# A mixture-of-experts loop on one core: where the weight splits, the stores and the activation table load stand

## The chip, the cores and the metric

The kernel runs on one core of a Trainium2 chip. The metric is device time in microseconds (us) of one execution, median of three runs. The core has five engines with queues of their own: TensorE (PE), VectorE (DVE), ScalarE (ACT), GpSimd (POOL) and SyncE (SP, which here only issues DMAs).

## The reference, cut to what matters

Three stages follow each other on 8 x 64 tokens of 512 features: cross attention to 8 x 1601 context rows, linear attention with a feed-forward layer, and a mixture of experts. The change is in the third:

```python
x = hidden_states.reshape(-1, h)                       # 512 tokens, 512 features
top_w, top_i = jax.lax.top_k(x @ w_router, 2)          # two of 8 experts each
gating = zeros.at[token, top_i].add(softmax(top_w))
for ei in range(8):
    hmid = silu(x @ w0[ei]) * (x @ w1[ei])             # 512 -> 1024
    out = out + gating[:, ei:ei + 1] * (hmid @ wo[ei]) # 1024 -> 512
```

All data is float32.

## The kernel before

**Numbers.** PE multiplies a value in two parts: an upper part (`_hi`, a Copy on ACT to the float32r type) and a lower part (`_lo`, the difference, a subtraction on DVE or POOL). A full product is three matmuls: hi x hi, lo x hi, hi x lo (`product`, lines L1535, L1538, L1539). To "split" a weight unit means to make both parts from the raw tile.

**Units.** An expert has six weight units of 128 x 2048 values (1 MB): j = 0 to 3 are the halves of `w0` and `w1`, j = 4 and 5 those of `wo`. Each has a raw tile and two parts. The tiles of units 0, 1 and 2 are those that the layer before used, so the trace calls them `w_raw`, `w_hi`, `w_lo` 1, 2 and 0; those of units 3 to 5 are `e_raw`, `e_hi`, `e_lo`. `split_e` exists on ACT (L774, upper part), DVE (L1271, lower part) and POOL (L549, lower part).

**Blocks.** The 1024 pairs of token and expert are scattered by POOL (L561) to an array `slots_x` in DRAM, in slots of 32 rows by expert. Each expert ends in one long block of 128 rows; what it has beyond that is done ahead of it in short blocks of 32 rows. How many there are is data: the engines read it into registers at the head of each expert (`expert_blocks`, L328) and loop over it. In this data experts 0, 3 and 5 have one short block, expert 2 has three, the others none. A short block multiplies the raw weights in 32-row strips (L2016) and needs no parts. A long block uses the parts.

**Order on PE.** Long block (`expert_block`): units 0, 1, 2, transposes of the first hidden half (L2000), unit 3, one quarter of unit 4, transposes of the second half, transposes of the next block's rows (L1986), the rest of unit 4, unit 5. Short block: units 0, 1, 2, a transpose (L2028), unit 3, the next rows, a transpose, units 4 and 5. The first product waits for the rows' lower part, each unit for its own parts; unit 4 waits for the lower part of the first hidden half (`hmT_lo`, made by `lower_hidden`, L1445), which DVE makes after `hidden` (L1441), the product of silu and the other half.

**Order on the others.** In the long block of expert e, ACT and DVE split the units of expert e + 1 in the order 0 to 5; DVE makes the lower parts of 0 to 4, POOL that of 5. SP loads a unit of the expert after next as soon as its lower part is made (L450); unit 0 also waits until the long block has begun (`raw_free`), since short blocks read raw tiles. The first expert's units 4, 5 and 1 are split by POOL during the feed-forward layer. ACT also stores each block's result to `slots_y` in four DMAs (L884 and L853) and waits for its own copy first:

```python
                act.wait_ge(y_ready, b + 2)
                row = row_of(b) * R
                for q in range(FULL_R):
                    nc.scalar.dma_start(ys[bass.ds(row + q * R, R), :], yb[q * R:(q + 1) * R, :]).then_inc(y_stored, 16)
```

The next copy into `yb` (L840) waits for `y_stored`. The silu of a block (L826) is preceded by a load of the activation table wherever the compiler does not know which table is in place; at the head of a loop it does not.

**The end.** When all earlier blocks are stored (`prior_stored`), POOL gathers each token's two results (L571) into `yt`, whose tiles lie over `e_raw` 3 and 4, so it also waits for the lower parts 3 and 4 of the last expert. DVE adds them (`gathered_added`, L1461 and L1462), the last block's rows reach the tokens by matmuls (L2086), `last_added` (L1519) adds those, and SP stores.

## Time and profile before

| | |
|---|---|
| median of 3 runs | 681.96 us (681.34 to 682.69) |
| profiled execution | 680.1 us, its span 678.1 us |
| PE busy | 623.4 us, 92% |
| DVE, ACT, POOL busy | 61%, 57%, 36% |
| granted TensorE clock, mean | 0.974 of full |
| expert loops | from about 437 us to the end |

The span runs from the first to the last instruction. A row of the timeline gives the start in us from the span's start, the duration, the engine, the line and operation, output<-inputs, the count merged into it, and in brackets the idle time of the engine before it and who ended it. "issue" means that the engine waited for nothing that the profile shows. PE's records overlap, since matmuls are pipelined: one start to the next is what counts.

### The profile page before, as it was taken

What the parts mean: (1) busy time and instruction counts of PE and PEld (TensorE: products, weight loads), DVE (VectorE), ACT (ScalarE), POOL (GpSimd) and SP (SyncE); (2) the same over time, 40 slices, a digit from 0 to 9 for tenths busy, and PEclk for the clock granted to TensorE, in tenths of its full rate; (3) what the DMA queues carried; (4) which work ended last, traced back from release to release, by engine and by line L of the source; (5) the groups of instructions that cost most, each with busy time, mean ns of one, the idle gap of its engine ahead of it and who ended that gap; (6) DMA issues with size and microseconds to landing.
All of it is one profiled execution on the core that took longest, in us unless ns stands there. A gap on an engine that the chain in (4) does not pass through costs nothing.

```text
span 678.1 us, 12394 instructions
## 1 busy us (share of the span) xinstructions
PE 623.4 (92%) x4593; PEld 508.5 (75%) x4594; DVE 416.2 (61%) x718; ACT 386.6 (57%) x567; POOL 245.0 (36%) x170
## 2 busy tenths in 40 slices
PE   8989999999989999899999999879966979979986
PEld 7867888888868888677888888768755758757764
DVE  7775667657767456667683447817731354764796
ACT  4589989979953344420432443427843556765760
POOL 4069987878963222340000223510220020220222
PEclk9999999999999999999999999979978979979999
DMA  8515653442423332499953310239911839939944
GB/s 316 211 63 194 203 186 133 165 154 71 139 80 88 125 109 103 156 398 388 375 181 119 125 63 0 94 131 358 368 35 21 332 103 353 360 103 338 360 154 152
DMA packets 57272, 125.54 MB, mean 185 GB/s; under 512 B 5896, under 2 KB 6664, under 8 KB 54160
## 3 DMA queue, kind: packets, MB, share of 16 engines
q1 hardware_dynamic: 51584, 115.16, 47.3%
q10 hardware_dynamic: 4368, 5.64, 2.8%
q0 software_dynamic: 1280, 4.20, 1.9%
q8 instruction: 26, 0.43, 0.3%
q14 instruction: 14, 0.11, 0.0%
HBM read 102.83 MB, written 22.15 MB: 184 GB/s over the span
## 4 chain that ended last, share of the span: by engine, by line
PE 69%; issue 8%; ACT 7%; DVE 6%; ACTq 4%; POOL 3%; DMA 1%; DVEq 0%; SPq 0%; POOLq 0%
PE bank L1535 14%; PE bank L1539 14%; PE bank L1538 14%; PE bank L1551 5%; PE bank L2016 3%; PE bank L1602 3%; POOL nat_lo L501 3%; PE bank L1603 2%; PE bank L1570 2%; PE bank L1571 2%; ACT e_hi L774 2%; ACTq L884 2%; PE bank L2000 1%; ACT nat_hi L618 1%; DVE hm L1441 1%
## 5 line engine op out<-in xcount | busy, mean ns | idle before, releaser
L501 POOL TENSOR_TENSOR nat_lo<-raw,nat_hi 128x512 fp32r<-128x512 f32 x104 | 136.1, 1339 | 41.8 <-ACT nat_hi L618 41.7
L549 POOL TENSOR_TENSOR e_lo<-e_raw,e_hi 128x2048 fp32r<-128x2048 f32 x8 | 36.6, 4576 | 223.4 <-ACT e_hi L774 223.4
L925 DVE TENSOR_TENSOR ct_lo<-bank,ct_hi 128x512 fp32r<-128x512 f32 x96 | 65.9, 689 | 33.2 <-ACT ct_hi L585 32.8
L618 ACT ACTIVATE nat_hi<-raw 128x512 fp32r<-128x512 f32 x104 | 64.7, 630 | 0.0
L585 ACT ACTIVATE ct_hi<-bank 128x512 fp32r<-128x512 f32 x96 | 57.0, 596 | 9.0 <-PE bank L1551 6.8
L1441 DVE TENSOR_TENSOR hm<-bank,vectors 128x512 f32<-128x512 f32 (+1 forms) x28 | 14.5, 519 | 75.9 <-PE bank L1539 35.7
L1271 DVE TENSOR_TENSOR w_lo<-w_raw,w_hi 128x2048 fp32r<-128x2048 f32 (+1 forms) x24 | 54.6, 2298 | 9.1 <-ACT w_hi L774 9.1
L1551 PE MATMUL bank<-ident,raw 128*128 128x128 f32 x384 | 57.7, 273 | 0.3
L1551 PEld LDWEIGHTS bank<-ident,raw 128*128 128x128 f32 x384 | 46.7, 140 | 12.8 <-issue 0.9
L1535 PE MATMUL bank<-turned,w_hi 128*128 128x512 f32 (+1 forms) x144 | 53.2, 370 | 1.4 <-DVE turned L1076 1.4
L1535 PE MATMUL bank<-w_hi,turned 128*128 128x512 f32 x128 | 50.7, 396 | 2.6 <-issue 2.5
L1539 PE MATMUL bank<-turned,w_lo 128*128 128x512 f32 (+1 forms) x144 | 52.8, 367 | 0.0
L1538 PE MATMUL bank<-turned,w_hi 128*128 128x512 f32 (+1 forms) x144 | 52.7, 366 | 0.0
L1602 PE MATMUL bank<-nat_hi,pT 128*128 128x512 f32 x104 | 48.6, 467 | 1.6 <-POOL nat_lo L501 1.1
L1539 PE MATMUL bank<-w_hi,turned 128*128 128x512 f32 x128 | 49.9, 390 | 0.0
L1538 PE MATMUL bank<-w_lo,turned 128*128 128x512 f32 x128 | 49.9, 390 | 0.0
L774 ACT ACTIVATE e_hi<-e_raw 128x2048 fp32r<-128x2048 f32 x24 | 45.8, 1909 | 6.8 <-issue 6.8
L774 ACT ACTIVATE w_hi<-w_raw 128x2048 fp32r<-128x2048 f32 x24 | 46.0, 1916 | 5.2 <-issue 3.6
L523 POOL TENSOR_TENSOR w_lo<-w_raw,w_hi 128x2048 fp32r<-128x2048 f32 x6 | 27.6, 4602 | 55.8 <-ACT w_hi L672 55.8
L1535 PE MATMUL bank<-e_hi,turned 128*128 128x512 f32 x96 | 39.6, 412 | 4.1 <-DVE turned L1445 4.1
L1603 PE MATMUL bank<-nat_lo,pT 128*128 128x512 f32 x104 | 40.9, 393 | 0.0
L1570 PE MATMUL bank<-ct_hi,pw_all 128*128 128x512 f32 x96 | 39.4, 410 | 1.4 <-DVE mx L937 1.4
(292 smaller groups left out, 1484.4 us busy)
## 6 DMA issues: line engine op xcount, KB each, us to landing
raw<-in_ctx_dram SPq DMA_DIRECT2D x24, 1024.0 KB, 5.0
w_raw<-in_L_ffn_w_dram SPq DMA_DIRECT2D x24, 1024.0 KB, 7.5
e_raw<-in_L_ffn_wo_dram SPq DMA_DIRECT2D x16, 1024.0 KB, 12.7
w_raw<-in_L_attn_w_dram SPq DMA_DIRECT2D x8, 1024.0 KB, 5.8
slots_x<-zeros SPq DMA_DIRECT2D x1, 8192.0 KB, 27.7
slots_y<-zeros SPq DMA_DIRECT2D x1, 8192.0 KB, 33.1
e_raw<-in_L_ffn_w_dram SPq DMA_DIRECT2D x8, 1024.0 KB, 11.6
vectors<-slots_x ACTq DMA_DIRECT2D x13, 256.0 KB, 4.6
```

Of the source, the lines that this page charges most:

```text
L501: nc.gpsimd.tensor_tensor(nat_lo[:, j, :], raw[b % 2][:, j, :], nat_hi[:, j, :].bitcast(f32), ALU.subtract).then_inc(nat_lo_ready, 1)
L585: nc.scalar.activation(ct_hi[:, n % CR, :], src, ACT.Copy).then_inc(t_hi, 1)
L618: nc.scalar.activation(nat_hi[:, j, :], raw[b % 2][:, j, :], ACT.Copy).then_inc(nat_hi_ready, 1)
L774: nc.scalar.activation(e_hi[j][:, :, :], e_raw[j][:, :, :], ACT.Copy).then_inc(e_hi_ready[j], 1)
L925: nc.vector.tensor_tensor(ct_lo[:, n % CR, :], src, ct_hi[:, n % CR, :].bitcast(f32), ALU.subtract).then_inc(t_lo, 1)
L1271: low = nc.vector.tensor_tensor(e_lo[j][:, rows_, :], e_raw[j][:, rows_, :], e_hi[j][:, rows_, :].bitcast(f32), ALU.subtract)
L1535: mm = nc.tensor.matmul(dst, lh, rh, start=first and k == 0, stop=False)
L1538: nc.tensor.matmul(dst, lh, rl, start=False, stop=False)
L1539: mm = nc.tensor.matmul(dst, ll, rh, start=False, stop=last and k == n - 1)
L1551: mm = nc.tensor.transpose(TB[n % 3][:, i * P:(i + 1) * P], raw[b % 2][:, CH * (g // CH) + i, (g % CH) * P:(g % CH + 1) * P], ident[:, :])
L1602: nc.tensor.matmul(value_bank(b)[:, :], pT[:, j, :], nat_hi[:, j, :], start=j == 0, stop=False)
L1603: nc.tensor.matmul(value_bank(b)[:, :], pT[:, j, :], nat_lo[:, j, :], start=False, stop=j == NKT - 1).then_inc(v_step, 1)
```

## The change

- POOL splits nothing of the experts but unit 1 of the first; DVE makes all other lower parts.
- In a long block of expert e, ACT and DVE now split units 4 and 5 of expert e itself, DVE also 2 and 3 of e, and of expert e + 1 DVE makes only 0 and 1 and ACT 0 to 3. This holds for the last expert's block too.
- SP stores a long block's result, in one DMA, after it has issued the next loads; ACT stores a short block's in one DMA instead of four.
- ACT runs a silu on four columns ahead of the loops.
- Short blocks wait for the loads of raw units, not for their upper parts.
- Ahead of the loops DVE makes the four lower parts of the first rows together, and no longer splits units 2 and 3 there; the gates of the last block are made after the first `lower_hidden`.

```diff
-        POOL_FIRST = (4, 5, 1)
+        POOL_FIRST = (1,)
...
                     load_unit(e, j)
+                last_b = sp.value_load(blocks[0:1, 1, bass.ds(e - 1, 1)], min_val=0, max_val=NB - 2)
+                row = sp.value_load(place_of[0:1, bass.ds(last_b, 1)], min_val=0, max_val=ROWS - FULL_R)
+                sp.wait_ge(y_ready, last_b + 2)
+                sp.dma_start(ys[bass.ds(row * R, P), :], yb[:, :]).then_inc(y_stored, 16)
...
-            with pool.Fori(1, E - 1) as e:
-                split_e(e, POOL_UNIT)
...
-                if n in (9, 10, 11):
-                    split_e(0, (4, 5, 3)[n - 9], (xT_done, 2 * KD))
+                if n == 11:
+                    split_e(0, 3, (xT_done, 2 * KD))
...
-                act.wait_ge(y_stored, 16 * FULL_R * b + 1)
+                act.wait_ge(y_stored, 16 * b + 1)
...
-                for q in range(FULL_R):
-                    nc.scalar.dma_start(ys[bass.ds(row, R), q * P:(q + 1) * P], yb[q * R:(q + 1) * R, 0:P]).then_inc(y_stored, 16)
+                nc.scalar.dma_start(ys[bass.ds(row, R), :].rearrange("t (q c) -> q t c", q=FULL_R), yb[:, 0:P]).then_inc(y_stored, 16)
...
                 silu(b, 0)
                 if last:
-                    act.wait_ge(y_stored, 16 * FULL_R * b + 1)
+                    act.wait_ge(xg_loaded, 16 * b + 16)
+                    act.wait_ge(y_stored, 16 * b + 1)
                     nc.scalar.activation(drained[:, :], mhalf[:, :], ACT.Copy).then_inc(prior_stored, 1)
+                split_e(e, 4)
+                split_e(e, 5)
                 split(0)
                 silu(b, 1)
                 upper_hidden(b, 0)
                 split(1)
+                split(2)
                 upper_hidden(b, 1)
...
-                split(2)
                 split(3)
                 output_copied(b, D)
-                split(4)
-                act.wait_ge(y_ready, b + 2)
-                row = row_of(b) * R
-                for q in range(FULL_R):
-                    nc.scalar.dma_start(ys[bass.ds(row + q * R, R), :], yb[q * R:(q + 1) * R, :]).then_inc(y_stored, 16)
-                split(5)
...
+            nc.scalar.activation(drained[:, :], mhalf[:, 0:NT], ACT.Silu)
             act.wait_ge(slots_ready, 5)
...
-            for k in range(2, KD):
-                first_lower_rows(k)
-            split_e(0, 2)
...
+                split_e(e, 2)
+                split_e(e, 3)
                 hidden(b, 0)
...
+                split_e(e, 4)
+                split_e(e, 5)
+                lower_hidden(b, 0)
+                if last:
                     gates_made()
-                split(0)
-                lower_hidden(b, 0)
                 hidden(b, 1)
                 if last:
                     gathered_added(0)
+                split(0)
                 lower_hidden(b, 1)
                 if last:
                     return
                 lower_rows(b + 1)
                 split(1)
-                split(2)
-                split(3)
-                split(4)
-
-            split_e(0, 3)
...
-            split_e(E - 1, 5)
...
-                pe.wait_ge(e_hi_ready[j], turn_of(e, j))
+                pe.wait_ge(e_loaded[j], 16 * turn_of(e, j))
```

DVE's order in a long block, before (`hm0`, `hm1`: the two hidden halves; `turned` from banks 4 and 5: `lower_hidden`; from bank 7: `lower_rows`):

```order
L1441 TENSOR_TENSOR hm0<-bank1,vectors 128x512
L1271 TENSOR_TENSOR w_lo1<-w_raw1,w_hi1 128x2048
L1445 TENSOR_TENSOR turned<-bank4,turned 128x512
...
L1441 TENSOR_TENSOR hm1<-bank3,vectors 128x512
L1445 TENSOR_TENSOR turned<-bank5,turned 128x512
```

and with the change, from the head of the block:

```order
L1271 TENSOR_TENSOR w_lo0<-w_raw0,w_hi0 128x2048
...
L1271 TENSOR_TENSOR e_lo3<-e_raw3,e_hi3 128x2048
...
L1438 TENSOR_TENSOR hm0<-bank1,vectors 128x512
L1271 TENSOR_TENSOR e_lo4<-e_raw4,e_hi4 128x2048
L1271 TENSOR_TENSOR e_lo5<-e_raw5,e_hi5 128x2048
L1442 TENSOR_TENSOR turned<-bank4,turned 128x512
```

Two splits now stand ahead of `hm0`, two between it and the lower part that PE's unit 4 waits for, and the split of the next expert's unit 0 (`w_lo1`) has moved behind `hm1`.

ACT at the end of a short block and the head of a long one, before:

```order
L853 DMA slots_y<-yb 32x128
...
L894 UNCONDITIONAL_BRANCH
...
L826 ACT_TABLE_LOAD
L826 ACTIVATE vectors<-bank0 128x512
...
L774 ACTIVATE w_hi1<-w_raw1 128x2048
```

and with the change:

```order
L855 DMA slots_y<-yb 4x32x128
...
L894 UNCONDITIONAL_BRANCH
...
L829 ACTIVATE vectors<-bank0 128x512
...
L777 ACTIVATE e_hi4<-e_raw4 128x2048
L777 ACTIVATE e_hi5<-e_raw5 128x2048
...
L777 ACTIVATE w_hi1<-w_raw1 128x2048
```

The table load is gone from both loops (it stands once, ahead of them), four stores are one, and two splits of the block's own expert stand ahead of the next expert's first.

SP, in its loop over the experts, a piece of the difference:

```order
 L450 DMA e_raw5<-in_L0_ffn_wo_dram 128x4x512
+L466 ISA
+L466 TENSOR_LOAD blocks
+L466 ISA x2
+L467 ISA
+L467 TENSOR_LOAD place_of
+L467 ISA x2
+L468 REGISTER_ALU
+L469 ISA
+L469 DMA slots_y<-yb 128x512
```

The store of the long block stands behind the last load of an expert, and ahead of the next expert's first.

## Rows read from the trace of the kernel before

**Rows 1.** windows: us, busy us by engine (instructions), clock, DMA share, GB/s

```profile
497.00:509.00 12.00, 8.89 (x198) 7.42 (x198) 1.28 (x3) 3.51 (x9) 3.68 (x1) 0.74 0.10 27
...
520.00:529.00 9.00, 6.97 (x114) 5.48 (x115) 1.28 (x3) 2.83 (x8) 0.00 (x0) 1.00 0.15 38
```

**Rows 2.** waits of PE from 437 to 678 us: in total, times, longest

```profile
PE bank L2028 <- DVE hm L1441: 22.3, 6, 4.6
```

**Rows 3.** timeline of PE: the first instruction of seven blocks

```profile
490.71 2.83 PE L2016 MATMUL bank<-w_raw,in_last 128*32 128x128 f32 x96
...
526.21 0.50 PE L1535 MATMUL bank<-w_hi,turned 128*128 128x512 f32 x1
...
544.69 2.06 PE L2016 MATMUL bank<-w_raw,in_last 128*32 128x128 f32 x68
...
558.63 0.50 PE L1535 MATMUL bank<-w_hi,turned 128*128 128x512 f32 x1
...
577.04 0.39 PE L1535 MATMUL bank<-w_hi,turned 128*128 128x512 f32 x1
...
596.90 0.86 PE L2016 MATMUL bank<-w_raw,in_last 128*32 128x128 f32 x24
...
651.41 0.47 PE L1535 MATMUL bank<-w_hi,turned 128*128 128x512 f32 x1 [2.50 <-issue]
```

**Rows 4.** timeline of ACT (ACTq: its DMA issues): between two blocks

```profile
496.11 1.28 ACT L826 ACT_TABLE_LOAD   x1
...
505.65 1.87 ACTq L853 DMA_DIRECT2D slots_y<-yb  x4
...
507.92 1.28 ACT L826 ACT_TABLE_LOAD   x1 [3.06 <-issue]
```

**Rows 5.** timeline of PE: a transpose in the third short block of expert 2

```profile
521.54 0.33 PE L2028 MATMUL bank<-ident,hm 128*128 128x128 f32 x1 [2.90 <-DVE hm L1441]
```

**Rows 6.** one line of a tile each: ns, minimum/median/maximum

```profile
L1271 DVE TENSOR_TENSOR e_lo<-e_raw,e_hi x16: 2284/2286/2289, 439.6 to 654.3; 128x2048 fp32r<-128x2048 f32 x16
...
L774 ACT ACTIVATE e_hi<-e_raw x24: 1896/1908/1926, 383.6 to 652.3; 128x2048 fp32r<-128x2048 f32 x24
```

**Rows 7.** timeline of POOL, DVE and PE in the long block of expert 1

```profile
476.57 4.62 POOL L549 TENSOR_TENSOR e_lo<-e_raw,e_hi 128x2048 fp32r<-128x2048 f32 x1 [33.88 <-ACT e_hi L774]
...
480.22 3.11 DVE L1271 TENSOR_TENSOR w_lo<-w_raw,w_hi 128x2048 fp32r<-128x2048 f32 x1 [1.02 <-ACT w_hi L774]
...
484.08 0.47 PE L1535 MATMUL bank<-e_hi,turned 128*128 128x512 f32 x1 [1.37 <-DVE turned L1445]
```

**Rows 8.** the scatter's line of POOL, in ns

```profile
L561 POOL DMA_INDIRECT slots_x<-xn,slot_all x8: 960/1122/2382, 429.8 to 440.8; - x8
```

**Rows 9.** timeline of PE: the next rows in the first short block

```profile
447.70 1.11 PE L1986 MATMUL bank<-ident,vectors 128*128 128x128 f32 x4 [0.75 <-DMA vectors<-slots_x]
```

**Rows 10.** timeline of DVE and PE in the last block

```profile
657.17 0.69 DVE L1441 TENSOR_TENSOR hm<-bank,vectors 128x512 f32<-128x512 f32 x1 [0.56 <-PE bank L1539]
...
659.86 0.16 DVE L1451 TENSOR_SCALAR gap<-gsum 128x4 f32<-128x4 f32 x1
...
661.01 0.69 DVE L1445 TENSOR_TENSOR turned<-bank,turned 128x512 fp32r<-128x512 f32 x1
...
663.95 0.66 PE L2000 MATMUL bank<-ident,hm 128*128 128x128 f32 x4 [0.15 <-DVE hm L1441]
...
671.28 0.74 DVE L1461 SCALAR_TENSOR_TENSOR xt<-yt,gate,xt 128x512 f32<-128x512 f32 x1
```

**Rows 11.** the gathers' line of POOL, in ns, and their landing

```profile
L571 POOL DMA_INDIRECT yt<-slots_y,slot_all x8: 942/947/1453, 656.0 to 665.7; - x8
...
DMA to landing us min/median/max: 3.5/3.7/4.0
```

**Rows 12.** DMA issues, 440 to 678 us: count, KB, us to landing

```profile
e_raw<-in_L_ffn_wo_dram SPq DMA_DIRECT2D x14, 1024.0 KB, 13.7
...
slots_y<-yb ACTq DMA_DIRECT2D x24, 16.0 KB, 4.9
```

More of the change, by code:

```diff
@@ L769, in _, with split_e @@
             act.wait_ge(b1_loaded, 16)
-            def split_e(e, j, wait):
+            def split_e(e, j, wait=None):
                 act.wait_ge(e_loaded[j], 16 * turn_of(e, j))
-                act.wait_ge(*wait)
+                if wait is not None:
+                    act.wait_ge(*wait)
                 nc.scalar.activation(e_hi[j][:, :, :], e_raw[j][:, :, :], ACT.Copy).then_inc(e_hi_ready[j], 1)
@@ L1417, in _ @@
             nc.vector.tensor_copy(blocks[:, 1, :], upto_extra[:, :]).then_inc(slots_ready, 1)
-            for k in range(2):
+            for k in range(KD):
                 first_lower_rows(k)
@@ L2030, in short_down @@
             def short_down(b, e, half):
-                pe.wait_ge(e_hi_ready[4 + half], turn_of(e, 4 + half))
+                pe.wait_ge(e_loaded[4 + half], 16 * turn_of(e, 4 + half))
                 pe.wait_ge(hmT_hi_ready, 2 * b + half + 1)
```

## The prediction

> **What bounds the kernel now.** I read the page's busy shares first, then the windows of the expert loops, PE's waits there, and the timelines around each wait. PE is busy 92% of the span, so only the stretches in which it is not can give time. From 437 us on they are of four kinds.
>
> First, short blocks. PE waits 22.3 us for `hm` ahead of the first transpose of six short blocks [rows 2], 4.6 us where a long block came before. The windows show the second cost: a granted clock of 0.74 of full around the first short block of expert 2, 1.00 in the third [rows 1]. So one short block with its idle costs 558.63 - 544.69 = 13.9 us, and the three of expert 2 cost 526.21 - 490.71 = 35.5 us [rows 3]. Their work at full clock is less: the first three units take 2.83 us [rows 3], and from the first transpose to the end of the block it is 526.21 - 521.54 = 4.7 us [rows 3, 5]; together 7.5 us.
>
> Second, a long block behind a long block takes 596.90 - 577.04 = 19.9 us, one behind a short block 577.04 - 558.63 = 18.4 us [rows 3]. Row 484.08 shows most of the difference: PE waits 1.37 us for `lower_hidden`, because DVE's split ahead of it takes 3.11 us beside POOL's split [rows 7], where it takes 2.29 us otherwise [rows 6]. That occurs three times (experts 1, 4, 6).
>
> Third, the first short block waits for its next rows until 447.70 [rows 9]. They come by the scatter, and one scatter instruction took up to 2.38 us where 1.12 us is the median [rows 8]; the slow two lie beside DVE's splits ahead of the loops.
>
> Fourth, the end: the last block and the gathers.
>
> I make the sum against the profiled execution, 680.1 us around a span of 678.1 us. The median of the runs, 681.96 us, lies 1.9 us above; I take the difference from the median. A change of less than 0.2% (1.4 us) could not be told from none.
>
> **Short blocks.** Behind a long block ACT copies the result, splits unit 4, issues four stores, splits unit 5 and loads the table at 496.11, 5.4 us after PE began [rows 3, 4]. With the change the copy is ACT's last work there. Between short blocks, the four stores take 1.87 us and the table load starts 0.40 us behind them and takes 1.28 us [rows 4]. Now one store, taken as 0.4 us (a quarter is 0.47), and no load: silu comes 1.5 + 1.3 = 2.8 us earlier, and PE's wait of 2.90 us [rows 5] shrinks to 0.3 us at most. For the block behind a long one I keep 0.6 us, for reading registers at the head of the expert. PE then has no idle stretch above 0.6 us, and the clock should stay at its upper level (2.4 GHz) as in the window from 520 us. So 7.8 us a block, 8.1 us for the first of an expert. Expert 2: 35.5 - 23.7 = 11.8 us. Experts 3 and 5: 13.9 - 8.1 = 5.8 us each, the second by the pattern of the first. Together **-23.4 us**. Bounds: 7.5 us a block, or the third block as it is now, 2.83 + 2.90 + 4.7 = 10.4 us: 2.6 us more on five blocks, +13 us.
>
> The table load's end shows no further cost in rows 4 beyond its 1.28 us. The Trainium skill, "ScalarE: Activation LUTs", section "What ACT_TABLE_LOAD costs", gives 1.28 us for the load and 1.38 us more for a drain, 2.66 us in all. By that page silu would be a further 1.4 us early, and the sum the same, since then PE's own units end last.
>
> **Long blocks.** Per block DVE gets a sixth split: 6 x 2.29 = 13.7 us, with five hidden and lower steps of about 0.69 us 17.2 us of 18.4. It fits, but the order decides. Take S as PE's start. `hidden` comes at 657.17 - 651.41 = S + 5.8 [rows 3, 10]. Units 2 and 3 are split ahead of it: they start at the end of the block before, at about S + 0.8, and end at S + 5.4. Then `hm0` to S + 6.5, units 4 and 5 to S + 11.1, `lower_hidden` to S + 11.7. PE ends unit 3 at about S + 11.7: row 663.95 is S + 12.5, less 0.15 of wait and a quarter unit of 0.7. So PE waits 0.1 us. ACT needs silu at S + 2.9, splits 4 and 5 to S + 7.2 (1.91 us each [rows 6]), unit 0 of the next to S + 9.1, and its three later splits and copies end at about S + 18.9: nothing is late. Loads: a unit is loaded when its lower part exists, so units 4 and 5 are requested at S + 9 and S + 11 and need up to 13.7 us [rows 12], S + 25. ACT needs them at S + 18.4 + 3.5 and + 5.4. That 13.7 us is mostly queueing behind the units ahead, and the queue now is shorter, so I cost it at nothing, with 1 us as its bound in the three pairs. SP's store adds about 1.5 us before the next loads; they are needed first at S + 7. Without POOL's splits, the 3.11 us are 2.29 us. So every long block takes 18.45 us: 3 x (19.86 - 18.45) = **-4.2 us**. Bound: DVE or ACT late by 1.2 us in each of seven, +8.
>
> **Ahead of the loops.** DVE's two splits go, so the last two scatters take 1.1 us instead of up to 2.4 us: rows come some 2.2 us earlier. PE has finished earlier too and is idle longer, so the clock comes back later into the long block. Between -2.3 and +1 us; I take **-1.5 us**. The feed-forward layer had no PE wait that POOL's or ACT's two splits caused: nothing. SP's and PE's changed waits: nothing.
>
> **The last block.** It used to have no splits. `lower_hidden` came at 661.01, S + 9.6; 1.15 us of that were gates (from 659.86), which now come later, and 2 x 2.29 us come in: S + 13.0, done at S + 13.7. PE is ready at S + 11.7 and waits 2.0 us; then gates hold `hm1` back another 1.1 us. PE's path is 3.1 us later. Worse, the gathers write over raw units 3 and 4 and wait for the last expert's lower part 4. They started at 656.0 [rows 11], S + 4.6. Now part 4 is ready at S + 10.9, 6.3 us later. The last of them was issued at 665.7 and landed 3.7 us later, 669.4 [rows 11]; DVE used it at 671.28 [rows 10], so 1.9 us of the delay were slack. 4.4 us are left, and DVE's split of unit 5 beside the first gather may slow that as in rows 8. I take **+5 us**; bounds +3.1 and +9 (if the clock falls after the idle).
>
> **Sum.** -23.4 - 4.2 - 1.5 + 5.0 = -24.1 us: 656.0 us for a profiled execution and 657.8 us for the median.
>
> **Rivals.**
> - *The short blocks keep a wait.* Register reads and the branch lie between store and silu, and I see only their sum. If half of the bound stays, +6.5 us; all of it, +13 us: 664 to 671 us. A case of its own is that the table load is still there: against it, the listing of ACT shows none in the loops. 0.15 together.
> - *The single short store is slow.* It walks four column groups, and the next copy into `yb` waits for all of it. The four stores took 4.9 us to land [rows 12]; from store to next copy there will be some 6.3 us. If it took twice 4.9 us, 3.5 us would be lost in each of the two short blocks of expert 2 that another follows, and the clock perhaps: 665 us. 0.05. The Trainium skill, "DMA: Bandwidth & Descriptors", section "Why a DMA increments its semaphore by 16 and not by 1", says that a transfer is spread over the largest number of DMA engines up to 16 that divides the slowest dimensions of both sides; here that is 4. This speaks against the change, and nothing in the trace of before shows such a store.
> - *Splits arrive late in the long blocks*, +8 us: 666 us. For: DVE is filled to 93%. 0.12.
> - *The tail costs less or the clock gives more*: 653 us. 0.08.
> - *DVE becomes the bound; slower.* If a split takes 3.1 us instead of 2.29 us for another reason than POOL (ACT reads and writes the same tiles at the same time), DVE needs 6 x 3.1 + 3.5 = 22.1 us per long block, 3.7 us more than PE, seven times: +26 us, 684 us. The point where it decides is 24.1 / 7 = 3.4 us per block. Rows 6 speak against it: sixteen splits, all with ACT at work, between 2284 and 2289 ns. With the clock falling as well, 690 us or more. 0.04.
>
> **Numbers.** Forecast 0.56, within 654 to 662 us; the rivals 0.15, 0.05, 0.12, 0.08, 0.04. The range of 652 to 667 us takes in the forecast, the faster case, the slow store, the late splits and the lower half of the first rival. Faster: 0.95. Slower: 0.03, and 0.02 for no change, both from the last rival.
>
> **What would show it.** Right: no table load after the one ahead of the loops; PE's waits for `hm` in short blocks below 0.7 us, with a clock near 1.00; short blocks of 8 us and long ones of 18.5 us; the rows of the first short block at about 445.5; POOL's first gather about 6 us after where it was relative to the last block's start, and DVE waiting for the last one. Wrong: waits of PE for `lower_hidden` or for a unit's parts above 0.5 us in the seven earlier long blocks, ACT waiting for a stored block, or splits above 2.4 us.

## The result and the profile after

| | before | changed |
|---|---|---|
| median | 681.65 us (680.2 to 682.69, 4 runs) | 660.93 us (660.35 to 661.3, 4 runs) |
| ratio | | 0.9697, 95% interval 0.9677 to 0.9717 |
| profiled execution, its span | 680.1, 678.1 us | 661.3, 659.5 us |
| PE busy | 92% | 94% |
| granted clock, mean | 0.974 | 0.982 |

The changed kernel is 20.7 us faster by the medians, 18.6 us by the spans that the stages below are read from (the profiled execution of before, 680.1 us, lies below the runs above, that of the changed kernel is the slowest of its four); the forecast was 24.1 us.

Stages by PE's first instructions (the start of a block to the start of the next; the last pair is counted to the start of the last matmul in the loop, the last line to the end of the span; expert 2's long block, 18.5 us in both, is left out):

| stage | before | changed | difference | forecast |
|---|---|---|---|---|
| start to the first long block (with expert 0's short block) | 452.38 | 449.86 | -2.5 | -1.5 |
| short blocks: three of expert 2 | 35.5 | 24.0 | -11.5 | -11.8 |
| short blocks of experts 3 and 5 | 13.9 + 13.6 | 7.4 + 7.4 | -12.7 | -11.6 |
| pairs of long blocks: 0+1, 3+4, 5+6 | 38.3, 38.3, 38.0 | 38.0, 37.6, 37.4 | -1.7 | -4.2 |
| last matmul in the loop to the last block | 2.9 | 5.0 | +2.1 | 0 |
| last block to the end | 26.7 | 34.4 | +7.7 | +5.0 |

Waits of PE from 437 us on, the view of [rows 2]:

```profile
PE bank L1532 <- issue: 4.6, 1, 4.6
PE bank L1532 <- DVE turned L1442: 4.1, 4, 1.9
PE bank L2013 <- ACT in_last L838: 3.2, 6, 0.7
...
PE bank L2083 <- DVE y_lo L1521: 2.2, 1, 2.2
PE bank L2025 <- DVE hm L1438: 1.6, 2, 0.8
```

Of the 22.3 us for `hm` in short blocks 1.6 us are left. The largest is now one wait of 4.6 us that no semaphore ends, at the exit of the expert loop. It is called the entry idle below, since it stands ahead of PE's entry into the last block. In the long blocks behind long ones PE now waits for the second lower half, three times, here the longest:

```profile
484.86 0.48 PE L1532 MATMUL bank<-e_hi,turned 128*128 128x512 f32 x1 [0.85 <-DVE turned L1442]
```

PE's block starts, which answer to [rows 3]:

```profile
487.84 1.41 PE L2013 MATMUL bank<-w_raw,in_last 128*32 128x128 f32 x44
...
511.88 0.50 PE L1532 MATMUL bank<-w_hi,turned 128*128 128x512 f32 x1
...
530.33 0.86 PE L2013 MATMUL bank<-w_raw,in_last 128*32 128x128 f32 x24
...
537.73 0.50 PE L1532 MATMUL bank<-w_hi,turned 128*128 128x512 f32 x1
```

Three short blocks take 511.88 - 487.84 = 24.0 us, one takes 537.73 - 530.33 = 7.4 us. The windows of expert 2's first short blocks and its third, as in [rows 1], both show full clock:

```profile
494.00:506.00 12.00, 10.29 (x324) 9.19 (x326) 1.32 (x4) 2.40 (x9) 0.00 (x0) 1.00 0.17 49
505.00:511.00 6.00, 4.58 (x123) 3.50 (x118) 1.77 (x4) 1.76 (x6) 0.00 (x0) 1.00 0.04 12
```

ACT between two short blocks ([rows 4]): no table load, but one store that takes 1.13 us to issue, not the 0.4 us that I had put down.

```profile
495.44 0.28 ACT L843 ACTIVATE yb<-bank 128x128 f32<-128x128 f32 x1 [1.37 <-PE bank L2013]
496.51 1.13 ACTq L855 DMA_DIRECT2D slots_y<-yb  x1
498.01 0.45 ACT L829 ACTIVATE vectors<-bank 128x128 f32<-128x128 f32 x2 [2.29 <-issue]
```

The lines of the splits and of the scatter ([rows 6] and [rows 8]), in ns:

```profile
L1271 DVE TENSOR_TENSOR e_lo<-e_raw,e_hi x24: 2281/2284/2287, 450.7 to 637.7; 128x2048 fp32r<-128x2048 f32 x24
...
L565 POOL DMA_INDIRECT slots_x<-xn,slot_all x8: 956/960/1226, 430.1 to 439.4; - x8
```

All of DVE's splits take 2.28 us with POOL silent, and no scatter exceeds 1.23 us.

The last block ([rows 10], [rows 11]), DVE, PE and POOL:

```profile
632.91 0.69 DVE L1438 TENSOR_TENSOR hm<-bank,vectors 128x512 f32<-128x512 f32 x1 [8.32 <-PE bank L1536]
...
635.47 4.49 DVE L1271 TENSOR_TENSOR e_lo<-e_raw,e_hi 128x2048 fp32r<-128x2048 f32 x2
639.88 0.68 DVE L1442 TENSOR_TENSOR turned<-bank,turned 128x512 fp32r<-128x512 f32 x1
...
644.83 0.76 DVE L1458 SCALAR_TENSOR_TENSOR xt<-yt,gate,xt 128x512 f32<-128x512 f32 x1 [2.45 <-DMA yt<-slots_y,slot_all]
```
```profile
625.10 0.77 PE L1532 MATMUL bank<-w_hi,turned 128*128 128x512 f32 x1 [4.59 <-issue]
...
642.43 0.66 PE L1997 MATMUL bank<-ident,hm 128*128 128x128 f32 x4 [0.79 <-DVE hm L1438]
```
```profile
638.59 2.22 POOL L573 DMA_INDIRECT yt<-slots_y,slot_all  x1 [198.22 <-DVE e_lo L1271]
```

DVE idles 8.3 us ahead of the first hidden half and then makes two splits, 4.5 us, with PE waiting behind them. The first gather starts 13.5 us into the block (4.6 before) and takes 2.22 us, of which 1.4 us lie beside DVE's split; DVE then waits for what it brings. The clock is the other half, shown for the entry:

```profile
620.35:622.35 2.00, 0.16 (x1) 0.00 (x0) 2.00 (x2) 0.60 (x1) 0.00 (x0) 1.00 0.83 303
...
625.10:629.10 4.00, 4.00 (x10) 3.13 (x11) 0.00 (x0) 0.00 (x0) 0.00 (x0) 0.50 0.01 4
```

The granted clock is 0.50 of full, the lower of its two levels (1.2 GHz), in the first 4 us of the block: ten matmuls, where before there were 18 in as long a stretch. The first row says what stood ahead of it: for 2 us after PE's last matmul in the loop the DMA engines are 83% busy, 303 GB/s. Before, the same stretch was empty:

```profile
648.74:650.74 2.00, 0.17 (x1) 0.00 (x0) 2.00 (x2) 2.00 (x3) 0.00 (x0) 1.00 0.02 5
```

### The profile page after: what moved, and what is told of

Same layout as the page of the kernel before. It is cut to its first block, busy times and chain, and to the rows that moved or that the text cites. A ratio compares the mean times of both kernels' runs of the same rounds, so it can differ in the third digit from the quotient of the medians.

```text
span 659.5 us, 12277 instructions
## 1 busy us (share of the span) xinstructions
PE 620.6 (94%) x4593; PEld 503.2 (76%) x4594; DVE 429.6 (65%) x726; ACT 369.9 (56%) x556; POOL 206.7 (31%) x162
## 4 chain that ended last, share of the span: by engine, by line
PE 71%; DMA 6%; ACT 6%; DVE 5%; issue 5%; POOL 4%; ACTq 2%; SPq 1%; POOLq 0%; DVEq 0%
PE bank L1532 15%; PE bank L1536 14%; PE bank L1535 14%; PE bank L1548 5%; DMA w_raw<-in_L_ffn_w_dram 4%; PE bank L2013 4%; PE bank L1599 3%; POOL nat_lo L505 3%; PE bank L1600 2%; PE bank L1567 2%; PE bank L1568 2%; ACT nat_hi L620 1%; POOL yt L573 1%; PE bank L1775 1%; PE bank L1584 1%
## 5 line engine op out<-in xcount | busy, mean ns | idle before, releaser
L573 POOL DMA_INDIRECT yt<-slots_y,slot_all x8 | 9.4, 1170 | 200.4 <-DVE e_lo L1271 198.2
L1532 PE MATMUL bank<-w_hi,turned 128*128 128x512 f32 x128 | 51.7, 404 | 4.7 <-issue 4.6
L1271 DVE TENSOR_TENSOR e_lo<-e_raw,e_hi 128x2048 fp32r<-128x2048 f32 x24 | 54.1, 2284 | 0.0
L1271 DVE TENSOR_TENSOR w_lo<-w_raw,w_hi 128x2048 fp32r<-128x2048 f32 (+1 forms) x24 | 52.3, 2195 | 0.7 <-ACT w_hi L777 0.7
L1536 PE MATMUL bank<-w_hi,turned 128*128 128x512 f32 x128 | 50.6, 396 | 0.0
```

Source lines behind the costliest of these rows:

```text
L1271: low = nc.vector.tensor_tensor(e_lo[j][:, rows_, :], e_raw[j][:, rows_, :], e_hi[j][:, rows_, :].bitcast(f32), ALU.subtract)
L1532: mm = nc.tensor.matmul(dst, lh, rh, start=first and k == 0, stop=False)
L1536: mm = nc.tensor.matmul(dst, ll, rh, start=False, stop=last and k == n - 1)
```

## The experiments

Differences of medians below are ratios to the kernel before, taken times 681.65 us, since each group of runs had its own runs of before. Twelve kernels were run.

**e1: the long block's store on ACT.** My first theory put the longer entry and the waits in the pairs down to SP's store, which stands ahead of the next loads.

```diff
-                last_b = sp.value_load(...)
-                row = sp.value_load(...)
-                sp.wait_ge(y_ready, last_b + 2)
-                sp.dma_start(ys[bass.ds(row * R, P), :], yb[:, :]).then_inc(y_stored, 16)
...
                 output_copied(b, D)
+                act.wait_ge(y_ready, b + 2)
+                nc.scalar.dma_start(ys[bass.ds(row_of(b) * R, P), :], yb[:, :]).then_inc(y_stored, 16)
```

> The changed kernel, but ACT issues the long block's store (one DMA) behind its copy, and SP neither reads the registers for it nor issues it. Theory 1: SP's store stands ahead of the next expert's loads and holds them back by about 1.8 us; that makes ACT's splits late in the long blocks behind long ones, and loads now run up to PE's entry into the last block, where PE's idle stretch of 4.6 us (before: 2.5 us) is an instruction fetch that waits among their packets, and the clock falls behind it. Then this run gains 4 to 6 us on the changed kernel: entry idle back to about 2.6 us, unit 0 of the last block at full clock, two long blocks in a row 37.0 us instead of 37.6 us. Rival: the loads are late because DVE now makes the lower parts later and because the DMA queues are busy, and the longer idle at the entry has another cause; then 0 to +1 us, since ACT's issue only delays its silu.

Measured: 668.23 us (667.92 to 668.88), ratio 0.9811 (0.9789 to 0.9833), 7.8 us slower than the changed kernel. The theory gave the wrong sign. ACT and PE at the head of expert 3's short block:

```profile
532.51 0.60 ACT L839 ACTIVATE yb<-bank 128x512 f32<-128x512 f32 x1 [1.55 <-PE bank L1534]
533.90 0.38 ACTq L882 DMA_DIRECT2D slots_y<-yb  x1
536.37 0.45 ACT L825 ACTIVATE vectors<-bank 128x128 f32<-128x128 f32 x2 [3.26 <-issue]
```
```profile
537.12 0.33 PE L2023 MATMUL bank<-ident,hm 128*128 128x128 f32 x1 [1.97 <-DVE hm L1436]
```
```profile
537.10:541.10 4.00, 3.98 (x54) 3.11 (x58) 0.30 (x2) 1.04 (x3) 0.00 (x0) 0.57 0.00 0
```

From the end of the copy to the issue are 0.8 us, in which ACT waits for its own write and reads the row's register, the issue takes 0.4, and 2.1 us more go by to the silu. PE waits 1.97 us where it had no idle stretch, and the clock is 0.57 over the next 4 us. From the start of expert 2's long block to that of expert 3's it is 29.1 us instead of 25.9, the next stage with its pair 48.3 instead of 45.0. So it is worth 7.8 us that the store does not stand ahead of ACT's silu; I had costed it on SP only, for what it delays there. What the theory said of the loads is half true. ACT's waits for raw units, with the change and in e1:

```profile
ACT w_hi L777 <- DMA w_raw<-in_L_ffn_w_dram: 4.3, 7, 0.7
```
```profile
ACT w_hi L773 <- DMA w_raw<-in_L_ffn_w_dram: 0.3, 1, 0.3
```

They are all but gone without SP's store, so here it was that store that held the loads back. But PE's waits for the lower hidden halves in the long blocks behind long ones only fall from 2.2 to 1.5 us, and the three pairs are 1.3 us shorter together. The entry idle falls from 4.6 to 3.8 us only.

**e2: the last block's order.** In the last block ACT splits units 4 and 5 ahead of its silu, DVE all four ahead of the hidden half, with the gates ahead of the lower half.

```diff
                 split_e(e, 2)
                 split_e(e, 3)
+                if last:
+                    split_e(e, 4)
+                    split_e(e, 5)
                 hidden(b, 0)
                 if last:
...
-                split_e(e, 4)
-                split_e(e, 5)
-                lower_hidden(b, 0)
-                if last:
                     gates_made()
+                else:
+                    split_e(e, 4)
+                    split_e(e, 5)
+                lower_hidden(b, 0)
```

> The changed kernel, but in the last block alone ACT splits units 4 and 5 ahead of its first silu, DVE splits all four of its late units ahead of the first hidden half, and the gates are made ahead of the first lower half, as before the change. Theory 1: of the +9.8 us that the last block and its entry now cost, the late splits and the gathers that wait for them make the 7.7 us inside the block. With the splits of units 4 and 5 ahead of the hidden half, the lower half comes 4.6 us less late behind it, and the gathers start about 1 to 4 us earlier: -2 to -6 us, and the entry idle stays at 4.6 us. Rival: the block is longer because the clock falls at its entry and in its middle; then the order on DVE changes nothing, or costs up to 2 us because the hidden half itself comes later (4.6 us of splits now stand ahead of it).

Measured: 657.86 us (657.18 to 658.65), ratio 0.9658 (0.9635 to 0.9681), 2.7 us faster than the changed kernel. The last block to the end takes 30.3 us instead of 34.4 in the profiled executions (more than the medians differ by; the stretches ahead of it scatter); the entry idle is 4.5 us and the clock falls behind it as before. The gathers, which wait for the last splits, start 6.8 us into the block instead of 13.5:

```profile
632.62 0.97 POOL L573 DMA_INDIRECT yt<-slots_y,slot_all  x1 [192.24 <-ACT drained L870]
```

Both theories have a part: 4.1 us of the 7.7 were the order, and the splits cost nothing where DVE had been idle for 8.3 us.

**e3: the edits of e1 and e2 together.**

> Both edits together: ACT's store of the long block and the other order in the last block. Theory 1: the gains add, -6 to -11 us on the changed kernel, 650 to 655 us. Rival (neither edit touches the cause): within 1 us of the changed kernel.

Measured: 662.84 us (660.81 to 664.28), ratio 0.9721 (0.9694 to 0.9747): 6.1 us below e1 and 4.3 above e2. The order in the last block helps on both; with e1's sign wrong, the sum is not the one I expected.

**e4: the changed kernel without the silu ahead of the loops.**

```diff
-            nc.scalar.activation(drained[:, :], mhalf[:, 0:NT], ACT.Silu)
```

> The changed kernel without the silu ahead of the loops, so that the activation table is loaded again (1.28 us) ahead of the silu in every block. Theory 1: each of the six short blocks loses the 1.28 us, three of them (expert 2) also lose clock if PE's idle stretch of then 2.1 us brings it down; long blocks have slack on ACT: +6 to +9 us. Rival, the drain behind a load that the Trainium skill gives (2.66 us for the pair): +14 us or more. Rival, the table load is hidden beside PE's three units and the shorter store did everything: 0 to +2 us.

Measured: 670.84 us (670.09 to 671.21), ratio 0.9844 (0.9822 to 0.9866), 10.0 us slower. The load is back, twelve times from 448 us on, as in the kernel before:

```profile
L829 ACT ACT_TABLE_LOAD x12 | 15.4, 1283 | 20.5 <-issue 20.5
```

PE's waits for `hm` in short blocks are 7.8 us instead of 1.6, so 6.2 us are the loads' own time. Of the rest, 1.4 us are clock in expert 2's short blocks (0.88 instead of 1.00) and 0.8 us clock in units 0 to 2 of the last block; what is left is spread over the long blocks. No second 1.4 us is to be seen beside a load, which the silu follows within 0.02 us: 2.66 us a load would have added over 13 us in the five blocks. This one line is worth 10.0 us in the changed kernel, about half of what the whole change brings.

**e5: the kernel before with only that silu**, and **e6: with one store a block as well**, both on ACT.

```diff
-                act.wait_ge(y_stored, 16 * FULL_R * b + 1)
+                act.wait_ge(y_stored, 16 * b + 1)
...
-                for q in range(FULL_R):
-                    nc.scalar.dma_start(ys[bass.ds(row + q * R, R), :], yb[q * R:(q + 1) * R, :]).then_inc(y_stored, 16)
+                nc.scalar.dma_start(ys[bass.ds(row, P), :], yb[:, :]).then_inc(y_stored, 16)
```

> The kernel before with only the silu ahead of the loops. If the table load costs what the run without this silu says for the changed kernel (+9.9 us), this run should be 8 to 11 us faster than before: each of the six waits of PE for the first hidden half in short blocks is 1.28 us shorter, and the clock comes back earlier in expert 2. If the load was hidden while four stores stood ahead of it (ACT late anyway), the waits still shorten, since the load stands behind the stores. Only if ACT were not what PE waits for would it be 0 to 2 us.

> The kernel before with that silu and with one store a block instead of four, on ACT for long blocks too. Per consecutive short block 1.87 us of issue become about 1.1 us, per block behind a long one 1.87 us become 0.4 us: another 4 to 7 us beyond the silu alone, 664 to 670 us. The changed kernel's remaining steps (splits of units 4 and 5 moved, POOL's splits gone, the long store on SP) are then worth 3 to 9 us net of their cost in the last block. Rival: these steps are worth nothing net, and this run is at 661 us or below.

Measured: e5 672.16 us (671.43 to 673.8), ratio 0.9883 (0.9834 to 0.9933), 8.0 us faster than before; e6 669.24 us (666.55 to 671.06), ratio 0.9842 (0.9794 to 0.9891), 10.8 us faster. PE's waits for `hm` in short blocks, e5 and then e6, from 448 us on:

```profile
PE bank L2029 <- DVE hm L1442: 12.8, 5, 3.2
```
```profile
PE bank L2027 <- DVE hm L1440: 10.5, 5, 3.0
```

The stores alone bring 2.8 us, less than the 4 to 7 us expected. Between short blocks the wait fell as expected, by 0.8 us each (the single short store is 1.1 us of issue instead of 1.87). Behind a long block it fell by 0.2 us only, from 3.2 to 3.0, where I had put down 1.5: ACT was no longer last there. DVE and ACT in e6 at the head of expert 2, and DVE's row of the same step before:

```profile
490.61 4.49 DVE L1270 TENSOR_TENSOR e_lo<-e_raw,e_hi 128x2048 fp32r<-128x2048 f32 x2
495.01 0.28 DVE L1440 TENSOR_TENSOR hm<-bank,vectors 128x128 f32<-128x128 f32 x1
```
```profile
493.82 0.44 ACT L826 ACTIVATE vectors<-bank 128x128 f32<-128x128 f32 x2
```
```profile
497.80 0.29 DVE L1441 TENSOR_TENSOR hm<-bank,vectors 128x128 f32<-128x128 f32 x1 [1.53 <-ACT vectors L826]
```

Before, DVE was idle for 1.53 us until the silu came. In e6 the silu is done at 494.3 and DVE starts without an idle stretch, behind two splits of the next expert's units that end at 495.1. What is left behind each long block, splits ahead of the first hidden half on ACT and on DVE, goes only with the rest of the change; that is worth 9.9 us net of what it costs at the end. Of the 20.7 us the silu is thus some 8, the stores 3, the rest of the change (the moved splits and SP's store above all) 10, when they are added in this order.

**e7: half the loads.** From the second expert on, units 4 and 5 are loaded by half, so that less traffic runs at the loop's exit (5 MB an expert instead of 6). The results of experts 1 to 7 are other ones; instructions and waits are the same.

```diff
-                sp.dma_start(e_raw[j][:, :, :], expert_unit(e, j)).then_inc(e_loaded[j], 16)
+                if not isinstance(e, int) and j > 3:
+                    sp.dma_start(e_raw[j][:, 0:2, :], expert_unit(e, j)[:, 0:2, :]).then_inc(e_loaded[j], 16)
+                else:
+                    sp.dma_start(e_raw[j][:, :, :], expert_unit(e, j)).then_inc(e_loaded[j], 16)
```

> The changed kernel, but from the second expert on units 4 and 5 are loaded by half (512 KB each instead of 1 MB; the other half of the tile keeps the first expert's values, so results of experts 1 to 7 are other ones; all instructions and waits stay). Theory: PE's instruction fetch at the loop's exit waits among the packets of the last loads, which now run until after PE's last matmul of expert 6. With a third of a quarter of the traffic less they end before it: entry idle 4.6 us becomes 2.5 to 3 us, and unit 0 of the last block runs at full clock for longer; -2 to -5 us in all, of which up to 2 us may come from ACT no longer waiting for raw units in the long pairs. Rival: the idle is the loop's exit itself or the place of the code; entry idle stays at 4.6 us.

Measured: 658.76 us (657.12 to 660.17), ratio 0.9675 (0.9624 to 0.9725), 1.5 us below the changed kernel, an interval that holds no difference too. The trace says more, in the window behind PE's last matmul in the loop and in PE's row at the entry:

```profile
622.14:624.14 2.00, 0.16 (x1) 0.00 (x0) 2.00 (x2) 0.60 (x1) 0.00 (x0) 1.00 0.06 18
```
```profile
625.05 0.47 PE L1535 MATMUL bank<-w_hi,turned 128*128 128x512 f32 x1 [2.75 <-issue]
```

With the DMA engines empty (0.06) after PE's last matmul, the entry idle is 2.75 us instead of 4.59, and the three units behind it run at full clock (8.06 us from first to last start instead of 10.10). The first long block happens to start 1.0 us later in this trace; from there to the end it is 2.8 us shorter than the changed kernel's, one trace of each.

**e9: the load of one unit late.** The same without leaving work out: SP asks for the last expert's unit 5 only when ACT has copied the block before, and issues the last long store behind it.

```diff
-            with sp.Fori(1, E) as e:
+            with sp.Fori(1, E - 1) as e:
...
+            last_b = sp.value_load(blocks[0:1, 1, E - 2:E - 1], min_val=0, max_val=NB - 2)
+            for j in range(EU):
+                if j == 0:
+                    sp.wait_ge(raw_free, E - 1)
+                if j == 5:
+                    sp.wait_ge(y_ready, last_b + 2)
+                load_unit(E - 1, j)
...
```

> The changed kernel, but SP issues the load of the last expert's unit 5 only after ACT has copied the result of expert 6's block, that is after PE's last matmul in the loop (nothing else moves; the unit is needed some 15 us later). Theory: PE's fetch of the instructions behind the loop starts when the load packets ahead of it are through; with unit 5 out of the way they end some 2 us earlier, the entry idle falls from 4.6 to about 2.6 to 3 us, and the clock does not fall, or for a shorter time: -2 to -4 us. ACT's split of unit 5 may wait some 1 to 2 us for the load, which costs nothing unless DVE's lower half waits behind it: +0 to +1.5 us. Rival: the fetch waits for something else, entry idle 4.6 us, 0 to +1 us in all.

Measured: 659.03 us (657.29 to 660.83), ratio 0.9687 (0.9662 to 0.9712), 0.7 us below the changed kernel, which is within the intervals (from the first long block to the end, 2.3 us by the two traces). The entry, in the windows and in PE's timeline:

```profile
622.12:624.12 2.00, 0.17 (x1) 0.00 (x0) 2.00 (x2) 0.60 (x1) 0.00 (x0) 1.00 0.00 0
...
624.90:628.90 4.00, 3.96 (x11) 3.14 (x12) 1.46 (x1) 0.00 (x0) 0.00 (x0) 0.59 0.85 313
```
```profile
624.94 0.47 PE L1541 MATMUL bank<-w_hi,turned 128*128 128x512 f32 x1 [2.65 <-issue]
```

The idle went as expected, the clock did not: it fell behind 2.65 us of idle here and stayed up behind 2.75 us in e7. On the idle itself all runs agree, nearly in the order of the DMA share in the 2 us behind PE's last matmul in the loop:

| run | DMA share | entry idle, us |
|---|---|---|
| before; e7, e9, e10, e12; e5 | 0.00 to 0.07 | 2.4 to 2.75 |
| e6 | 0.18 | 3.0 |
| e3, e1 | 0.52, 0.61 | 3.7, 3.8 |
| e4, e2 | 0.71, 0.75 | 4.1, 4.5 |
| changed, e11, e8 | 0.83, 0.83, 0.93 | 4.6, 4.4, 4.5 |

In this stretch of each trace one packet of 16 KB of kind "instruction" is moved. It takes 1.0 to 1.4 us, and in all fourteen traces it is through 1.61 to 1.65 us before PE's first matmul of the last block. It is its start that differs: within 0.4 us of the end of PE's last matmul where the DMA share is 0.18 or less, 1.0 to 1.9 us behind it where the share is above 0.5 (622.4 us in the changed kernel, 1.9 us behind). So the fetch waits among the packets of the last loads, which run so late because units 4 and 5 are now split late, and asked for late.

**e8: all stores on POOL**, on top of e2. POOL's queue is empty in the loops. It waits for ACT's copy, stores, waits for the landing and signals by a subtraction on one column; ACT and SP issue no store.

```diff
+            def relay(b):
+                pool.wait_ge(pool_stored, 16 * b + 16)
+                nc.gpsimd.tensor_tensor(relayed[:, :], mhalf[:, 0:1], mhalf[:, 0:1], ALU.subtract).then_inc(y_stored, 1)
...
+                nc.gpsimd.dma_start(ys[bass.ds(row, R), :].rearrange("t (q c) -> q t c", q=FULL_R), yb[:, 0:P]).then_inc(pool_stored, 16)
+                relay(b)
```

> The version with the other order in the last block, and all stores on POOL, whose queue is empty in the loops: POOL waits for ACT's copy, reads the row, issues the store, waits until it has landed and signals by a subtraction on one column. SP's loads no longer stand behind a store, and ACT neither waits for its own copy nor issues. Theory: ACT's silu in the three short blocks that follow a short one comes 1.5 to 2.5 us earlier, so PE's remaining waits of 0.8 us there go, and the loads come 1.8 us earlier in long pairs: -2 to -5 us on the version without this edit, 653 to 656 us. Rival: POOL's path from copy to landing takes so long (over 6 us) that ACT's next copy waits for it in consecutive short blocks: +1 to +6 us.

Measured: 651.4 us (649.16 to 652.82), ratio 0.9578 (0.9528 to 0.9628): 5.5 us below e2. Against e2 it gains 2.3 us from the first long block to that of expert 2, 1.1 and 1.5 us in the stretches with the other two pairs, and 2.1 us in the last block (by the traces, of which e8's is its fastest execution). PE's waits from 448 us on:

```profile
PE bank L1562 <- issue: 4.5, 1, 4.5
PE bank L2043 <- ACT in_last L864: 2.9, 6, 0.6
...
PE bank L1562 <- DVE turned L1469: 1.0, 1, 1.0
PE bank L2027 <- DVE hm L1465: 0.2, 1, 0.2
```

Both waits of 0.8 us for `hm` are gone, and so are all waits for `turned` but one. The store lands in time between short blocks: POOL issues it in 0.72 us and signals 3.0 to 3.1 us after it began. Ahead of a long block, beside the loads, the signal comes only after 6.8 to 7.1 us, but no copy waits for it there:

```profile
495.81 0.74 POOL L573 DMA_DIRECT2D slots_y<-yb  x1 [4.46 <-issue]
498.84 0.19 POOL L568 TENSOR_TENSOR relayed<-mhalf 128x1 f32<-128x1 f32 x1 [2.29 <-DMA slots_y<-yb]
...
536.06 0.71 POOL L573 DMA_DIRECT2D slots_y<-yb  x1 [4.42 <-issue]
542.92 0.19 POOL L568 TENSOR_TENSOR relayed<-mhalf 128x1 f32<-128x1 f32 x1 [6.14 <-DMA slots_y<-yb]
```

The three pairs of long blocks are 4.1 us shorter together than in the kernel before. ACT still waits 2.7 us for raw units, in other places than before, of which one reaches PE. e8 moves the short stores and the long one at once, so what each of them gains was not measured.

**e11: DVE's order in every long block**, on top of e2: the split of the next expert's unit 0 behind the second lower half and the next rows.

```diff
-                split(0)
                 lower_hidden(b, 1)
...
                 lower_rows(b + 1)
+                split(0)
                 split(1)
```

> The version with the other order in the last block alone (not POOL's stores), with DVE's split of the next expert's unit 0 moved behind the second lower half and the next rows, in every long block. Theory: PE's waits of 0.8 us for the second lower half in the long blocks that follow a long one come from this split, which starts late because ACT waited for raw unit 0 of the next expert; they go (three times), and the next block's hidden half is just in time: -1.5 to -2.5 us. Rival: DVE has no slack in these blocks, and the split that now starts 1.5 us later returns as a wait for the next block's hidden half or lower half: 0 to +3 us.

Measured: 655.47 us (653.98 to 658.32), ratio 0.9654 (0.9619 to 0.9689), against 0.9658 for e2: no difference. DVE's row in the long block of expert 4 says why:

```profile
570.55 0.69 DVE L1446 TENSOR_TENSOR turned<-bank,turned 128x512 fp32r<-128x512 f32 x1 [2.90 <-ACT turned L833]
```

It is ACT that is late with the upper half, because it has waited 0.30 and 0.73 us for raw units of the next expert, which stand in the queue behind SP's store. In e8, where that store is gone, ACT waits 0.36 us for raw units in this block and PE not at all. My theory of this run named the wrong engine.

**e10 and e12: e8 with the late load of unit 5.** In e10 SP waits for ACT's copy, in e12 for POOL's signal that the result is stored. In the last block ACT splits unit 5 behind its first silu, DVE behind the first lower half.

```diff
-                    sp.wait_ge(y_ready, last_b + 2)
+                    sp.wait_ge(y_stored, last_b + 2)
```

> The version with all stores on POOL and the other order in the last block, with the same late load, and with unit 5 of the last expert split behind the first silu on ACT and behind the first lower half on DVE. Theory: its entry idle of 4.5 us becomes about 2.7 us, and units 0 to 2 of its last block, 9.6 us from first to last start, take 8.1 us at full clock: -3 us, about 648 us. Rival as for the run above: 0 to +1 us.

> As the run before with POOL's stores and the late load, but SP issues that load only when POOL has signalled that expert 6's result is stored. In that run the store took 5.8 us to land beside the load (2.0 us without it), so the gathers started 4 us later against the last block's start, and PE's last product waited 3.7 us for the sums. Theory: with the store first, the gathers start about 4 us earlier and the 2.1 us that were lost at the end come back, while the entry idle stays at 2.5 us: about 648 us. The load now lands some 6 us into the last block, in time for the split that stands behind the first lower half. Rival: the load is now late for that split or runs beside the gathers, and the end stays where it is: 650 to 652 us.

Measured: e10 650.85 us (650.34 to 651.54), ratio 0.9579 (0.9556 to 0.9601); e12 651.63 us (650.57 to 653.05), ratio 0.9576 (0.9547 to 0.9605); e8's was 0.9578. No gain in either, though the entry idle is 2.4 and 2.7 us as it should be. In e10 the store of expert 6 now runs beside the load; POOL's wait for its landing, 2.04 us in e8, is 5.79:

```profile
618.70 0.54 POOL L586 DMA_DIRECT2D slots_y<-yb  x1 [9.75 <-issue]
625.03 0.19 POOL L575 TENSOR_TENSOR relayed<-mhalf 128x1 f32<-128x1 f32 x1 [5.79 <-DMA slots_y<-yb]
```

The gathers wait for it and start 8.3 us into the block instead of 6.2 (2.1 us later, not the 4 us of the expectation above), one of them takes 2.39 us beside DVE's split of unit 5, and PE's last product waits 3.7 us. In e12 the load is what comes late: ACT waits for it, and the silu and upper half behind the split wait with ACT:

```profile
629.30 1.92 ACT L810 ACTIVATE e_hi<-e_raw 128x2048 fp32r<-128x2048 f32 x1 [5.14 <-DMA e_raw<-in_L_ffn_wo_dram]
```

The two microseconds won at the entry were lost again inside the block both times, to the same megabyte: from PE's last matmul in the loop to the end e8 takes 32.7 us, e10 32.1 and e12 34.2.

## Why the prediction was right, point by point

The sign, the size and the range held: 660.9 us within 652 to 667, inside the forecast case (654 to 662), 3.1 us above the point. By the two traces, on which the sum was made, the gain is 5.5 us short of the forecast: 7.3 us too little in the pairs, the last block and the entry, 1.8 us too much elsewhere. That the medians are only 3.1 us off is in part luck of which executions were profiled.

- **Short blocks, -23.4:** -24.2 us. The path was as described, table load gone, copy as ACT's last work behind a long block, clock at 1.00 throughout. Two errors cancelled in part: the store takes 1.13 us to issue and leaves a wait of 0.8 us instead of 0.3, so the two blocks of expert 2 that follow a short one take 8.4 us each, not 7.8; and a block behind a long one takes 7.3 or 7.4 us, not 8.1, since no wait for `hm` was left there. One thing the working did not see: it priced ACT's path alone. e6 shows that DVE's two splits alone would have kept a wait of 3.0 us behind a long block; the change moved them too.
- **Table load without a drain:** held, by e4. The Trainium skill, "ScalarE: Activation LUTs", section "What ACT_TABLE_LOAD costs", gives 2.66 us for load and drain. Here the load takes 1.28 us, no drain shows, and PE's waits grow by 6.2 us in five blocks, so in this kernel the measurement decides for the load alone. The silu is worth 8 to 10 us, more than the loads' time on PE's path; some 2 us of that are the clock's (e4), which the forecast held in one term with the rest.
- **Long behind long, -4.2:** -1.7 us. This step failed. DVE's split is 2.28 us as forecast, but "nothing is late" was wrong for ACT: the sentence that SP's store adds about 1.5 us before loads that are first needed at S + 7 was the right sum with the wrong conclusion. ACT waited 4.3 us in seven waits for them, and PE 2.2 us in three waits for the second lower half behind it. Without SP's store the pairs gain 3.0 us on the kernel before (e1), without any store on ACT or SP 4.1 us (e8), which is the forecast's size.
- **Ahead of the loops, -1.5:** -2.5 by the two traces. The first long block starts between 448.5 and 451.9 us in the eleven traces that share the changed kernel's code there (median 450.2) and at 451.3 to 452.4 in the three of the other (451.5), so -1.3 is the better reading, and this stretch alone scatters by 3 us. The step itself held: the last two scatters took 2.38 and 1.90 us in the three kernels that have DVE's splits beside them and 0.96 us in the eleven that have not, and the first rows landed at 445.4 us instead of 447.7, the 2.2 us of the forecast. How much of that PE gained is not settled: two of the three other kernels (e5, e6) have the silu ahead of the loops already.
- **The last block, +5:** +7.7, within its bounds of +3.1 and +9, which named the clock. PE waited 1.9 us for the lower half (2.0 forecast). 2.05 us are unit 0 to 2 at half clock, and 1.7 us the clock's second fall, after that wait, over the last quarter units (21 matmuls in 6.4 us instead of 4.7). The working also took the gathers' start as S + 10.9; it was S + 13.5, mostly because of the clock. But of the gathers' delay, from which the point of +5 was taken, only 0.7 us reached PE's last product (its wait for `y_lo` is 2.2 us instead of 1.6): the sum came near through PE's own waits and the clock.
- **The entry:** +2.1 us that no step named. The forecast costed the later loads only by when ACT needs them, and wrote that the queue was shorter. That they would be in the way of PE's own instruction fetch was not considered. e7 and e9 show it.
- **Rivals.** *The single short store is slow:* false. Its last packet is through 2.3 us after its issue began (at 496.51 us, between two short blocks) and no copy waits for it; four column groups are not a limit here, by whatever number of DMA engines it is spread. *The short blocks keep a wait:* true for 0.8 us in two of six. *Splits late in the long blocks:* true in small, 2.5 us of the 8. *The tail costs less:* false, it cost more. *DVE becomes the bound:* false, no split above 2.29 us.
- **The signs.** Of those for "right", the missing table loads, the rows at 445.4 us, the clock and DVE's waits for the gathers came; PE's waits for `hm` were 0.8 us instead of below 0.7, and the first gather 8.9 us later instead of 6. One sign for "wrong" came too: PE waited 0.85, 0.61 and 0.75 us for `lower_hidden` in three of the seven earlier long blocks, above the 0.5 us named. The total was right while that step was not.

What stays open: why the clock fell at the entry of e9 and e5 (2.65 and 2.6 us of idle) and not in e7, e10, e12 or before (2.4 to 2.75 us). It is worth 1.4 to 1.6 us a time. And in e2 and e3 DVE's second hidden half began 1.4 us later behind PE's unit than in e11 or before; nothing in the traces accounts for it.

The version that beats both kernels is e8: 651.4 us, ratio 0.9578, 29 us below the kernel before.

## What to carry to other kernels

Before an issue or a store is taken for cheap, ask what stands behind it on its engine: a store that takes 0.4 us to issue made the kernel 7.8 us slower when it moved from SP to ACT, ahead of a silu, and with all stores on an engine with an empty queue it was 5.5 us faster than with them on ACT and SP (e8 against e2). An activation function run once ahead of a loop can take the table load out of every pass. Where a transfer is moved, look at what runs beside it at its new place, an engine's instruction fetch at a loop's exit among it: here that was 2 us, and moving one megabyte once more only moved the collision.

## What the runs showed of the hardware that I had not expected

- PE's instruction fetch waits among data transfers. At the loop's exit PE stood still 2.4 to 2.75 us with idle DMA engines and up to 4.6 us with busy ones, in fourteen kernels, almost in the order of the DMA share, and always 1.61 to 1.65 us beyond the end of the 16 KB instruction packet.
- A store of 128 rows into a pattern of 4 x 32 rows x 128 columns took 1.06 to 1.20 us to issue on ACT, where the store of 128 x 512 in plain rows took 0.37 us; on POOL the two took 0.72 and 0.57 us.
- A gather of POOL took 0.95 us alone and 2.2 to 2.4 us beside a split on DVE (in the changed kernel and in e1, e4, e7, e9, e10 and e12); the scatters fell from up to 2.38 to 1.23 us at most when DVE's splits beside them went.
- PE idle stretches of 1.9 to 2.1 us inside short blocks were followed by the lower clock in e1 (three of three, 0.57 over 4 us), e4 (two of two) and e3 (two of three); of three of 3.0 us in e6 one was not. Behind stretches of 0.8 us it stayed at 1.00.
